# Router logits of a graph layer moved from TensorE products to eight running sums on VectorE, and two normalisations written as one

## What is computed

```python
x = x + gnn(_layernorm(x))
x = x + ffn(_layernorm(x)[None])[0]
...
logits = xt @ Wr + br
probs = jax.nn.softmax(logits, axis=-1)
top_p, top_idx = jax.lax.top_k(probs, 2)
weights = top_p / top_p.sum(axis=-1, keepdims=True)
mu = xt.mean(axis=-1, keepdims=True)
var = ((xt - mu) ** 2).mean(axis=-1, keepdims=True)
xn = (xt - mu) * jax.lax.rsqrt(var + LN_EPS)
```

## Time and profile before

| | |
|---|---|
| median of 3 runs | 2184.47 us (2181.71 to 2184.82) |
| profiled execution | 2183.68 us, its span 2182.0 us |
| TensorE busy | 1986.6 us, 91% of the span |
| VectorE busy | 1317.4 us, 60% |
| ScalarE busy | 819.5 us, 38% |
| L1506, the sums of layer two | 551.5 us busy, 2401 matmuls |
| layer two's sums, first to last | 881.8 to about 1481.7 us |
| sorting by expert | from 1501.4 us |
| first gather of the experts | 1547.6 us |

### The profile page before, as it was taken

How to read it: one execution, slowest core, us unless ns; L and a number is a source line. 1 busy time by engine, 2 the same in 40 slices (tenths; PEclk the granted TensorE clock), 3 DMA queues, 4 the chain that set the end, 5 groups by cost and what they waited for, 6 DMA issues and landing times. The chain is left out here.

```text
span 2182.0 us, 42240 instructions
## 1 busy us (share of the span) xinstructions
PE 1986.6 (91%) x14616; PEld 1323.0 (61%) x14617; DVE 1317.4 (60%) x2860; ACT 819.5 (38%) x1837; POOL 504.6 (23%) x636
## 2 busy tenths in 40 slices
PE   1489999999999995899999999994699999999997
PEld 1345555555555552455555555552599999999996
DVE  8876666676766761244444444446766666666664
ACT  4655555555555551011112121211344444444442
POOL 5720000000000001000000000000355566556653
PEclk9999999999999997899999999996799999999998
DMA  7022222222222221556464757554133323332322
GB/s 224 4 119 93 116 119 90 119 107 101 119 90 119 118 90 74 208 174 215 169 220 169 255 193 247 199 211 184 37 51 48 49 47 51 48 49 47 51 47 27
DMA packets 73720, 256.30 MB, mean 117 GB/s; under 512 B 9927, under 2 KB 50312, under 8 KB 59368
## 3 DMA queue, kind: packets, MB, share of 16 engines
q1 hardware_dynamic: 30520, 181.37, 22.0%
q0 software_dynamic: 28944, 60.16, 12.8%
q10 hardware_dynamic: 14112, 12.85, 1.7%
HBM read 139.26 MB, written 115.08 MB: 117 GB/s over the span
## 5 line engine op out<-in xcount | busy, mean ns | idle before, releaser
L662 PE MATMUL mp_o<-rows,m_counts 128*128 128x512 f16 x2401 | 601.0, 381 | 12.8 <-ACT m_counts L762 6.6
L1506 PE MATMUL rp_o<-rows,r_adj 128*128 128x512 f16 x2401 | 551.5, 380 | 34.3 <-DMA r_adj<-adj 34.3
L762 ACT ACTIVATE m_counts<-mp 128x490 f16<-128x490 f32 (+4 forms) x664 | 360.0, 560 | 350.9 <-PE mp L696 345.1
L1506 PEld LDWEIGHTS rp_o<-rows,r_adj 128*128 128x128 f16 x2401 | 235.7, 100 | 283.2 <-issue 38.0
L584 DVE TENSOR_TENSOR m_oh_lane<-lane_b,m_edge_lane 128x1920 f16<-128x1920 bf16 (+1 forms) x209 | 242.0, 1158 | 201.0 <-PE mp L696 199.2
L662 PEld LDWEIGHTS mp_o<-rows,m_counts 128*128 128x128 f16 x2401 | 209.2, 98 | 190.5 <-issue 15.1
L1998 PE MATMUL fp_h<-f_xt,w 128*128 128x256 f16 x2688 | 304.5, 274 | 0.3 <-DVE f_xt L2094 0.3
L2017 PE MATMUL fp_y<-w,f_hh 128*128 x2688 | 302.4, 273 | 0.0
L696 PEld LDWEIGHTS mp<-m_oh_cell,m_oh_lane 128*128 128x128 f16 x3125 | 202.3, 99 | 140.2 <-DVE m_oh_lane L584 19.8
L1998 PEld LDWEIGHTS fp_h<-f_xt,w 128*128 x2688 | 263.9, 98 | 31.4 <-issue 0.6
L2017 PEld LDWEIGHTS fp_y<-w,f_hh 128*128 128x128 f16 x2688 | 263.0, 98 | 30.4
(11 more groups left out here) (210 smaller groups left out, 1649.3 us busy)
## 6 DMA issues: line engine op xcount, KB each, us to landing
adj<-m_counts SPq DMA_DIRECT2D x49, 1568.0 KB, 5.2
r_adj<-adj SPq DMA_DIRECT2D x49, 1568.0 KB, 6.7
r_raw<-in_L_ffn_W_dram POOLq DMA_DIRECT2D x16, 1024.0 KB, 8.4
w_parts<-r_parts POOLq DMA_DIRECT2D x8, 1024.0 KB, 5.8
w<-w_parts SPq DMA_DIRECT2D x4, 2048.0 KB
rows<-in_x_dram SPq DMA_DIRECT2D x7, 896.0 KB, 12.5
r_x<-in_x_dram SPq DMA_DIRECT2D x49, 128.0 KB, 2.0
out_dram<-r_x ACTq DMA_DIRECT2D x49, 128.0 KB, 1.7
```

The source lines that it names most:

```text
L662: mm = nc.tensor.matmul(ps_o[q], counts[:, q, s, :], k.rows[0][:, s, :], start=i == 0, stop=i == BLOCKS - 1)
L762: last = nc.scalar.activation(counts[:, q, :, lo - b * P:hi - b * P].rearrange("p h (a d) -> p h a d", d=STEP), items[:, :, (lo - first_ds ...
L1506: mm = nc.tensor.matmul(ps_o[q], adj[:, q, s * P:(s + 1) * P], rows[:, s, :], start=s == 0, stop=s == BLOCKS - 1)
```

## The change

It takes `turn_norm`, `route` and ScalarE's copy of zt out of layer two. VectorE computes the logits itself: for each block eight `scalar_tensor_tensor` instructions multiply xn (128x256) with one router column, broadcast to all partitions, and keep the running sum of the product (`accum_out`); the product itself goes to a scratch tile, junk. The logits of block b - 1 (before: b - 2) are done behind `combine(b)`, ahead of the bias of block b.

Only one normalisation is carried out, x2 to xn. With m and v the mean and variance of x2, z = (x2 - m) / sqrt(v + eps), and the variance of z is v / (v + eps), so xn = (x2 - m) / sqrt(v (1 + eps) + eps^2). ScalarE takes both roots of the block's variance, one for each. The router's z is xn times the quotient of the roots, so `choose_two` scales the sums with that quotient and adds br, in three small instructions ahead of the rest.

The router weights come in transposed (`wr_rows`, 8x256), and their broadcast load (8 KB for each of 128 partitions) and that of br stand behind the second block's adjacency and x in SP's queue; before, wr (8 KB in all) and br stood ahead of the first adjacency. VectorE waits for them after the second `combine`.

```diff
-        wr = sb("_wr", [P, KF, EXPERTS], fp32)
+        wr = sb("_wr", [P, EXPERTS, D], fp32)
...
-        z = sb("_z", [P, 2, D], fp32)
         xn = sb("_xn", [P, 2, D], fp32)
-        zt = sb("_zt", [P, 2, D], fp32)
+        junk = sb("_junk", [P, EXPERTS, D], fp32)
...
+        sq = sb("_sq", [P, BLOCKS, 2], fp32)
+        rec = sb("_rec", [P, BLOCKS, 2], fp32)
+        ratio = sb("_ratio", [P, TOP_MOST], fp32)
+        eps2 = sb("_eps2", [P, 1], fp32)
...
-        STEPS = 4
-        WEIGHTS = 64
+        STEPS = 2
+        WEIGHTS = 32
...
-            sp.dma_start(wr[:], k.io["L0_ffn_Wr"].rearrange("(c p) n -> p c n", p=P)).then_inc(w_in, 16)
-            sp.dma_start(br[:], k.io["L0_ffn_br"][None, :].to_broadcast([P, EXPERTS])).then_inc(w_in, 16)
...
                 if b == 1:
+                    sp.dma_start(wr[:].rearrange("p e d -> p (e d)"),
+                                 k.io["wr_rows"].rearrange("e d -> (e d)")[None, :].to_broadcast([P, EXPERTS * D])).then_inc(wr_in, 16)
+                    sp.dma_start(br[:], k.io["L0_ffn_br"][None, :].to_broadcast([P, EXPERTS])).then_inc(wr_in, 16)
                     n = EXPERTS * KF
...
-            def turn_norm(b):
-                pe.wait_ge(zt_ready, b + 1)
-                if b:
-                    pe.wait_ge(t_copied, b)
-                for c in range(KF):
-                    mm = nc.tensor.transpose(ps_t[:, c * P:(c + 1) * P], z[:, b % 2, c * P:(c + 1) * P], k.ident[:])
-                mm.then_inc(t_done, 1)
-            def route(b):
-                pe.wait_ge(t_copied, b + 1)
-                if b:
-                    pe.wait_ge(logit, b)
-                for c in range(KF):
-                    mm = nc.tensor.matmul(ps_l, zt[:, b % 2, c * P:(c + 1) * P], wr[:, c, :], start=c == 0, stop=c == KF - 1)
-                mm.then_inc(l_done, 1)
             pe.wait_ge(w_in, WEIGHTS)
-            for b in range(BLOCKS + 2):
+            for b in range(BLOCKS + 1):
...
                         turn_over(b - 1)
                     if part == 2 and 1 <= b <= BLOCKS:
                         product(b - 1)
-                    if part == 3 and b >= 2:
-                        turn_norm(b - 2)
-                    if part == 4 and b >= 2:
-                        route(b - 2)
...
-            def copy_norm(b):
-                act.wait_ge(t_done, b + 1)
-                if b >= 2:
-                    act.wait_ge(l_done, b - 1)
-                nc.scalar.activation(zt[:, b % 2, :], ps_t, ACT.Copy).then_inc(t_copied, 1)
...
+            act.wait_ge(eps_set, 1)
...
-                if b:
-                    copy_norm(b - 1)
-                for t in range(2):
-                    act.wait_ge(var_ready, b * 2 + t + 1)
-                    nc.scalar.activation(mv[:, t, 1:2], mv[:, t, 1:2], ACT.Sqrt, bias=k.eps[:]).then_inc(root, 1)
+                act.wait_ge(var_ready, b + 1)
+                nc.scalar.activation(sq[:, b, 0:1], mv[:, q, 1:2], ACT.Sqrt, bias=k.eps[:])
+                nc.scalar.activation(sq[:, b, 1:2], mv[:, q, 1:2], ACT.Sqrt, bias=eps2[:], scale=1.0 + EPS).then_inc(root, 1)
                 act.wait_ge(x2_ready, b + 1)
                 act.dma_start(k.io["out"][b * P:(b + 1) * P, :], x2[:, q, :]).then_inc(x2_out[q], 16)
                 act.wait_ge(xn_ready, b + 1)
                 act.dma_start(k.xn_rows[b * P:(b + 1) * P, 0:D], xn[:, q, :]).then_inc(xn_out[q], 16)
-            copy_norm(BLOCKS - 1)
...
-            def norm(b, t, src, out, done):
-                nc.vector.bn_stats(stats[:, t, :], src).then_inc(step, 1)
-                dve.wait_ge(step, b * STEPS + 2 * t + 1)
-                nc.vector.bn_aggr(mv[:, t, :], stats[:, t, :]).then_inc(var_ready, 1)
-                dve.wait_ge(root, b * 2 + t + 1)
-                nc.vector.reciprocal(mv[:, t, 1:2], mv[:, t, 1:2]).then_inc(step, 1)
-                dve.wait_ge(step, b * STEPS + 2 * t + 2)
-                nc.vector.tensor_scalar(out, src, mv[:, t, 0:1], mv[:, t, 1:2], ALU.subtract, ALU.mult).then_inc(done, 1)
+            def norm(b):
+                q = b % 2
+                nc.vector.bn_stats(stats[:, q, :], x2[:, q, :]).then_inc(step, 1)
+                dve.wait_ge(step, b * STEPS + 1)
+                nc.vector.bn_aggr(mv[:, q, :], stats[:, q, :]).then_inc(var_ready, 1)
+                dve.wait_ge(root, b + 1)
+                nc.vector.reciprocal(rec[:, b, :], sq[:, b, :]).then_inc(step, 1)
+                dve.wait_ge(step, b * STEPS + 2)
+                nc.vector.tensor_scalar(xn[:, q, :], x2[:, q, :], mv[:, q, 0:1], rec[:, b, 1:2], ALU.subtract,
+                                        ALU.mult).then_inc(xn_ready, 1)
 
             def logits(b):
-                dve.wait_ge(l_done, b + 1)
-                nc.vector.tensor_tensor(k.logits[:, b, :], ps_l, br[:], ALU.add).then_inc(logit, 1)
+                dve.wait_ge(xn_ready, b + 1)
+                if b:
+                    dve.wait_ge(logit, b)
+                for e in range(EXPERTS):
+                    dot = nc.vector.scalar_tensor_tensor(junk[:, e, :], xn[:, b % 2, :], 1.0, wr[:, e, :], ALU.mult, ALU.mult,
+                                                         accum_out=k.logits[:, b, e:e + 1])
+                dot.then_inc(logit, 1)
...
                 dve.wait_ge(logit, e)
+                link(nc.vector.tensor_tensor(ratio[:, 0:m], sq[:, bs, 1], rec[:, bs, 0], ALU.mult))
+                link(nc.vector.tensor_tensor(k.logits[:, bs, :], k.logits[:, bs, :], bc(ratio[:, 0:m, None], full), ALU.mult))
+                link(nc.vector.tensor_tensor(k.logits[:, bs, :], k.logits[:, bs, :], bc(br[:, None, :], full), ALU.add))
                 for c in range(2):
...
+            nc.vector.memset(eps2[:], EPS * EPS).then_inc(eps_set, 1)
             dve.wait_ge(w_in, WEIGHTS)
...
                 combine(b)
-                if b >= 2:
-                    logits(b - 2)
+                if b == 1:
+                    dve.wait_ge(wr_in, 32)
+                if b:
+                    logits(b - 1)
...
-                    dve.wait_ge(t_done, b - 1)
                 nc.vector.scalar_tensor_tensor(x2[:, q, :], pre[:, q, :], 0.0, x[:, q, :], ALU.max, ALU.add).then_inc(x2_ready, 1)
                 dve.wait_ge(x2_ready, b + 1)
-                norm(b, 0, x2[:, q, :], z[:, q, :], zt_ready)
-                dve.wait_ge(zt_ready, b + 1)
-                norm(b, 1, z[:, q, :], xn[:, q, :], xn_ready)
-            logits(BLOCKS - 2)
+                norm(b)
             weigh(len(TOP_ENDS) - 2)
             logits(BLOCKS - 1)
...
+    arrays["wr_rows"] = _np.ascontiguousarray(arrays.pop("L0_ffn_Wr").T)
```

More of the change, by code:

```diff
@@ L1413, in build_layer_two @@
         ps_h = pb("p_h", [P, D], fp32)
-        ps_t = pb("p_t", [P, D], fp32)
-        ps_l = pb("p_l", [P, EXPERTS], fp32)
         ps_s = pb("p_s", [P, (2 * KF + HB) * EXPERTS], fp32)
         (w_in, summed, half, agg_ready, agg_t_done, agg_copied, h_done, pre_ready, x2_ready, step,
-         var_ready, root, zt_ready, xn_ready, t_done, t_copied, l_done, logit, zero_set, zero_out) = (
+         var_ready, root, xn_ready, logit, zero_set, zero_out) = (
             sem("_" + s) for s in ("w_in", "summed", "half", "agg", "agg_t", "agg_copied", "h", "pre", "x2",
-                                    "step", "var", "root", "z", "xn", "t_done", "t_copied", "l_done", "logit", "zero_set",
+                                    "step", "var", "root", "xn", "logit", "zero_set",
                                     "zero_out"))
+        wr_in, eps_set = sem("_wr_in"), sem("_eps_set")
         raw_in, w_hi, w_lo, w_out, small_in, small_t, top, gap_ready, exp_done, gates_ready, gates_out = (
```

## The result

The kernel after takes 2157.72 us (median of 4 runs, 2156.81 to 2158.37) against 2183.91 us for the kernel before (4 runs): a ratio of 0.9881 with a 95% interval of 0.9864 to 0.9898, 26.2 us less. The profiled execution has a span of 2155.8 us, where that of before had 2182.0.

What follows compares the result with a forecast made beforehand. TensorE's full queue was taken to bound layer two, VectorE only its end. Stream -27.3, start -0.9 and end +5.4 sum to -22.8 us, giving 2160.9 or 2161.7 by baseline; forecast 2161.5 us, range 2157 to 2168.

Steps and rivals of the forecast that it cites:

- a gain beyond 26 us: Whole kernel: the outcome of a larger saving than forecast, given a chance of 0.02.
- TensorE's slots: TensorE's stream in layer two: z's turn and router product go, 0.58 us a block, 47 pairs, gain 27.3 us.
- Both readings of the rows: TensorE's timeline: removed slots 0.21 plus 0.37 us; period without them 11.66 against some 12.24; both give 0.58 us.
- The cover: VectorE in layer two's stream: the dots fit its idle time, agg's turns don't wait; lateness up to 2.6 us costs nothing.
- The end: Last sum to gates, VectorE the path: 15.7 us becomes 21.1, a loss of 5.4 us (4.4 to 6.2).
- the dot: VectorE's 256-element product with running sum: 0.46 us each, bounds 0.40 to 0.51; eight take 3.68 us.
- the free start of combine: VectorE after a block's last sum: combine starts about 0.30 us after that sum's end, an estimate.
- The start: Layer two's first loads: two small loads leave the queue ahead of the first adjacency, gain 0.9 us (0 to 1.5).
- Rival A: VectorE's dots run at half rate, 2.08 ns an element, 0.73 us each: net -18, 2166 us; chance 0.10.
- Rival B: Adjacency loads pace some blocks because later low halves delay weight transfers: 4 to 8 us, 2167 us; chance 0.08.
- Rival C: VectorE becomes the stream's bound: slower than before from 0.86 us a dot; at 0.99, +50, 2234 us; chance 0.03.
- Rival D: Removing the pairs leaves TensorE's stream unshortened, bubbles remain; only start and end count: +4.5, 2189 us; chance 0.02.

Runs made afterwards that it cites:

- e10: The kernel after, unchanged, run again on another chip beside fresh runs of the kernel before: 2164.56 us, ratio 0.9889.
- e1: Kernel after with the removed turn and router product's fp32 work put back on TensorE in 47 blocks, on constant weights, unread: 2186.74 us, ratio 1.0017.
- e3: Kernel after with sixteen running sums per block instead of eight, the second eight unread: 2166.49 us, ratio 0.9922.
- e4: Kernel after with twenty-four running sums per block instead of eight, sixteen of them unread: 2251.21 us, ratio 1.0308.
- e9: Kernel after with the choices of the two largest logits ending at blocks 45 and 49 instead of 47 and 49: 2161.25 us, ratio 0.9871.
- e6: Kernel after with unread VectorE probes (products without sum, one-source sums, plain products) behind blocks 5, 20 and 35: one run, mean period 11.710 us.
- e8: Kernel after with sixteen running sums per block and the weights' low halves moved ahead of them: 2171.11 us, ratio 0.9919.

## Why the prediction was right

It named the right bound, the right price of the stream and the right sign at each place; the time came 3.8 us below the forecast and 0.7 above the lower edge of the range. That it lies inside is in part luck. The forecast's own range, 2158 to 2164.5, does not hold 2157.72, and a gain beyond 26 us, which is what was measured, had been given a chance of 0.02. Two terms missed in the same direction, the end by 2.2 us and the start by 1.2, of which the second is scatter; on the chip of e10 the gain was 24.7 us. Point by point:

- **TensorE's slots**: -27.3 worked out, -27.2 in the profile, and e1 puts them back, period by period. The agreement to 0.1 is closer than its parts. The last of the 47 router products stood behind the last sum, so 46 pairs and one turn, 26.9, was the count for this stretch; the periods and the last turn gave 26.8, and 0.4 came from the scatter before the first turn. Both readings of the rows had given the 0.58, the block without norm and route above all.
- **The cover**: VectorE idle before combine and before the bias; turns of agg without a wait; the chain back to combine early enough. e3 shows how far VectorE's part of it reaches (with sixteen dots TensorE still never waits for VectorE in the stream), e4 that it ends, with a mean period that the sum of VectorE's work tells to 0.1 us.
- **The end**: +5.4 worked out, +3.2 measured. This is the term that was mis-sized, and in it the dot: 0.46 us where 0.345 was measured, sixteen times 0.115 = 1.8 of the 2.2 us. The range for a dot, 0.40 to 0.51, did not hold it. Its step was to take the fixed part, 0.19, from the instructions with a running sum in layer one, whose inputs are 16-bit integers; and the lower end, 0.40, from combine, which reads PSUM. A nearer row stands in the timeline of VectorE before, at the kernel's beginning, and was not used:

```profile
21.05 2.38 DVE L457 BATCH_NORM_STATS2 m_stats<-rows 128x6 f32<-128x256 f32 x7
```

Seven independent statistics of 128x256 fp32 in 2.38 us, each 0.41 long, so (2.38 - 0.41) / 6 = 0.33 from start to start. The rest of the 2.2 is 0.1 us each from the free start of combine (0.2 after the slot, not 0.3), choose_two, the chain from the bias to weigh, and weigh.
- **The start**: -0.9 worked out, -2.1 between the two profiles. The issue is 1 us earlier, as worked out; what lies beyond is scatter, as the twelve lags show. A single pair of profiles would have put all of it down to the change.
- **Rival A** fell: two fp32 sources with a running sum take 0.345 us, without one 0.336, and 1.04 ns an element and a fixed 0.07 fit both. The Trainium skill, Vector Engine (DVE) Microarchitecture Reference, section Points that are easy to get wrong, says that this form with two non-bf16 SBUF sources "halves throughput". It does not say against what; read as 2.08 ns an element, as rival A took it, no run here shows it, with or without the sum, and the measurement decides.
- **Rival B** did not happen, but was nearer than its chance says: the longest landing rose from 8.8 to 9.3 us (up to 10.0 in e9) against a period of 11.66, and 2.9 us more of delay made it happen (e3).
- **Rival C** did not happen at eight dots and did at twenty-four, 3 us above the 2248 that e4's expectation had summed (where the stream came 2.4 us lower and the end 3.4 higher). **Rival D** is refuted by e1 and by the period.
- The sum with what was measured in each place is -27.2 - 1.0 + 3.2 = -25.0, or -26.1 with the start as the two profiles have it; the medians differ by 26.2 here and by 24.7 on the chip of e10.

## What to carry to other kernels

Where one engine's queue is full, the gain of moving work off it is the slots between the neighbours' starts, and it could be read here to a percent from a block that lacks that work (0.58 us a pair forecast, 26.6 us over 46 pairs measured). The work's price then lies where the receiving engine has no idle time left, mostly behind the last block, and what else stands there (a choice, a weighing) should be moved ahead of it. A step that moves back in its block takes the transfers that follow it along: compare the longest landing with the period, not the median.

## What the runs showed of the hardware that was not expected

- Independent VectorE instructions of 128x256 fp32 from SBUF start 0.336 us apart though each lasts 0.42 (e6); a running sum adds 0.01, its read of 0.08 being hidden. Where each waits for the one before, it is 0.46.
- The first adjacency of layer two feeds the first sum 9.27 to 10.69 us after its issue, over nine profiles of kernels that issue the same transfers in the same order up to there.
- TensorE kept a mean granted clock of 0.97 in a stage where it waited for VectorE 24 times, 1.7 us each in the mean (e4).
- One chip ran the kernel before in 2189.2 us, where it took 2181.6 to 2183.9 in the other sets. The profiles of the three kernels from there (e8, e9, e10) begin layer two 5.3 to 6.3 us later than the first profile of the kernel after; the kernel before was not profiled there.
